# Layer 3's label masks made transposed, counted on TensorE, and scaled after the product on VectorE

## The chip, the cores and the metric

One Trainium2 chip, one core. The metric is the device time of one execution in microseconds (us). The kernel before took 1689.04 us, the median of three runs (1688.54 to 1689.13).

## The reference

A graph network of four layers runs on 64 graphs. Each graph has 128 nodes with 256 features, and an integer adjacency matrix of 128x128 that all layers share. Layers 0 and 2 are attention with eight heads, layer 1 is attention with one head, and each layer ends in a layer norm. The change is in layer 3, which sums neighbours by label, projects the sums and runs a gated unit:

```python
labels = jnp.arange(1, D + 1, dtype=adj.dtype)                  # D = 4 labels
mask = (adj[None] == labels[:, None, None, None]).astype(dt)
weight = mask / (jnp.sum(mask, axis=-1, keepdims=True) + EPS)
agg = jnp.einsum('dbmn,bnh->bmdh', weight, hid).reshape(hid.shape[0], hid.shape[1], D * H)
out = jax.nn.relu(_linear(agg, Wd, bd))
r = jax.nn.sigmoid(_linear(out, Wri, bri) + _linear(hid, Wrh, brh))
z = jax.nn.sigmoid(_linear(out, Wzi, bzi) + _linear(hid, Wzh, bzh))
n = jnp.tanh(_linear(out, Wni, bni) + r * _linear(hid, Wnh, bnh))
out = (1.0 - z) * n + z * hid                                   # then a layer norm
```

Row m of a label's mask is divided by its own sum, and this factor depends only on m. So it can be applied to the mask before the product, or to row m of the product.

## The kernel before, in words

**Rounds.** Two graphs (G = 2) are one pair, and 32 pairs run as 32 rounds of a software pipeline. Every engine has an order written out by hand (`ORDER`, with the function `periods`). An entry `lab.2@4` is part 2 of the step `lab`, run in a period for the pair that is four behind. Each engine runs its list once per period in that order, and semaphores alone tie the engines to one another. The lists of two engines may begin at different points of the round. An engine that waits holds back all that stands behind it in its list; SP's list holds the DMAs.

**Number forms.** Most products are made in fp32r, from a high and a low part of each operand, which takes three products (hi by hi, hi by lo, lo by hi). Products in plain fp32 stand in the trace as two TensorE instructions each. Transposes are products with an identity.

**Layer 3 before.** `mask` (VectorE, L990) makes the four 0/1 masks of both graphs in E3 with nodes m on partitions. `cnt` (VectorE, L995) sums rows, `guard` adds the epsilon, `rcnt` takes the reciprocal, and `wm` (GpSimd, L827) multiplies the masks by it. `wt.0` and `wt.1` transpose the weighted masks on TensorE (L577), ScalarE copies them out to wT (L740). `lab.0` to `lab.3` (TensorE, L590) multiply the node features by the label's part of Wd, for one graph and two labels each, into the banks B3 and A3 in turn; ScalarE copies each to xw (L747). `out` (TensorE, L599) multiplies xw by wT in plain fp32 and sums the four labels in bank A3; ScalarE adds the bias and applies relu (L752), and VectorE splits the result into high and low parts (L1005, L1008). `nh`, `rh`, `ri`, `ni`, `z` are the projections of the gates, and `mixt` transposes the mixed result.

**What stands around it.** `s02.0` and `s02.1` are the scores of layers 0 and 2 together (L403): four heads' worth of banks A0, B0, A2, B2 are filled at each. `s02.1` waits until ScalarE has read the four banks of `s02.0` (`exp0.1`, `exp2.1`); before that VectorE masks each bank (`fill`, L889), takes row maxima (`max`, L892, L968), and ScalarE exponentiates in four pieces (`exp`, L666, L727). `v0` projects layer 0's values, ScalarE adds their bias (L651), and `vb0` (L452) transposes them. `p0`, `p2`, `p1` transpose attention weights; `hop0`, `hop2` (L417) apply them; `back0` (L491) and `n1`, `n2`, `n3` (L391) are transposes; `vo1` and `v2` are at L385.

## Time and profile before

| | |
|---|---|
| median of 3 runs | 1689.04 us |
| the profiled execution | 1689.4 us, its span 1687.6 us |
| TensorE (PE) busy | 1619.2 us, 96% of the span |
| ScalarE (ACT) busy | 1205.6 us, 71% |
| VectorE (DVE) busy | 1130.4 us, 67% |
| GpSimd (POOL) busy | 782.0 us, 46% |
| mean granted TensorE clock | 0.985 of full speed |

The span is the time from the first to the last instruction, and the execution's time is 1.8 us longer. Busy shares are means over filling, steady rounds and draining. "PEld" is TensorE's weight load, which overlaps its products. Durations of neighbouring instructions on one engine overlap a little, so what an instruction costs in a stream is the distance from its start to the next one's start; the chain of waits gives such distances.

### The profile page before, as it was taken

Reading aid. Unit: us, or ns where it says so; the run is one execution under the profiler, and the core shown is the slowest. Engines: PE = TensorE matmul, PEld = TensorE weight load, DVE = VectorE, ACT = ScalarE, POOL = GpSimd, SP = SyncE. Lnnn points to the kernel's source line nnn. Section 1 sums busy time; section 2 is a strip of 40 time slices with the busy share of each in tenths; the row PEclk is TensorE's granted clock in tenths of the full one; section 3 lists DMA queues with packets and bytes.
Section 4 is the critical chain, followed back from the end, with each engine's and each line's share of the span. In section 5 each row is a group of like instructions: output and inputs, shape, how many; then the busy total and the mean of one; then the engine's idle time right before and its main releaser. Section 6 shows DMA issues by size and latency. Waiting matters only on the chain.

```text
span 1687.6 us, 44431 instructions
## 1 busy us (share of the span) xinstructions
PE 1619.2 (96%) x17552; PEld 1488.0 (88%) x17552; DVE 1130.4 (67%) x2875; ACT 1205.6 (71%) x4008; POOL 782.0 (46%) x774
## 2 busy tenths in 40 slices
PE   4788999999999999999999999999999999999985
PEld 3677999999999999999999999999999999999885
DVE  3566666677766676766667676666767666677642
ACT  4477777777777777777777777877778777777542
POOL 1345454534554454455544455454445554544521
PEclk8899999999999999999999999999999999999997
DMA  5000000110011111001101101111110111100000
GB/s 191 17 23 27 26 27 30 33 33 23 15 32 33 30 33 33 17 21 33 33 30 32 33 6 32 33 30 33 33 33 5 33 33 30 33 27 17 20 7 13
DMA packets 71135, 51.51 MB, mean 31 GB/s; under 512 B 4368, under 2 KB 69904, under 8 KB 70288
## 3 DMA queue, kind: packets, MB, share of 16 engines
q1 hardware_dynamic: 70928, 48.66, 9.5%
q8 instruction: 140, 2.29, 0.6%
q14 instruction: 67, 0.55, 0.1%
HBM read 40.26 MB, written 8.39 MB: 29 GB/s over the span
## 4 chain that ended last, share of the span: by engine, by line
PE 91%; issue 3%; DVE 3%; ACT 2%; POOL 1%; DMA 1%; SPq 0%; POOLq 0%; DVEq 0%; ACTq 0%
PE bank_A L373 15%; PE bank_B L373 10%; PE bank_A L599 7%; PE bank_B L590 5%; PE bank_A L590 5%; PE bank_A L417 5%; PE bank_B L417 4%; PE bank_A L403 4%; PE bank_C L411 3%; PE bank_C L373 3%; PE bank_X L373 3%; PE bank_B L385 3%; PE bank_X L385 3%; PE bank_X L525 2%; PE bank_A L391 2%
## 5 line engine op out<-in xcount | busy, mean ns | idle before, releaser
L795 POOL TENSOR_TENSOR E<-E,rsum 128x512 f32<-128x512 f32 x256 | 276.5, 1085 | 302.7 <-DVE rsum L896 181.8
L803 POOL TENSOR_TENSOR rstd<-var,minus_half 128x2 f32<-128x2 f32 x128 | 90.6, 708 | 219.4 <-DVE var L931 219.4
L373 PE MATMUL bank_A<-xT_hi,w_hi 128*128 128x256 f32 x512 | 139.4, 294 | 13.7 <-DVE xT_lo L866 11.5
L818 POOL TENSOR_TENSOR xn<-y,row 128x512 f32<-128x512 f32 x64 | 82.8, 1294 | 124.1 <-DVE y L983 122.5
L373 PE MATMUL bank_A<-xT_hi,w_lo 128*128 128x256 f32 x512 | 134.0, 283 | 0.0
L783 POOL TENSOR_SCALAR absent<-absent 128x256 int32<-128x256 int32 x64 | 57.3, 895 | 162.0 <-DMA absent<-in_adj 154.3
L889 DVE COPY_PREDICATED_SCALAR bank_A<-absent,fill 128x512 f32 x128 | 92.4, 743 | 44.7 <-PE bank_B L403 43.8
L599 PE MATMUL bank_A<-wT,xw 128*128 128x128 f32 x1024 | 119.6, 275 | 0.0
L599 PEld LDWEIGHTS bank_A<-wT,xw 128*128 128x128 f32 x1024 | 116.9, 192 | 0.0
L690 ACT ACTIVATE xT_hi<-bank_A,col 128x256 fp32r<-128x256 f32 x128 | 65.2, 561 | 71.0 <-PE bank_A L391 71.0
L964 DVE TENSOR_TENSOR vnat<-bank_B,row 128x512 f32<-128x512 f32 x32 | 22.1, 691 | 132.9 <-PE bank_B L385 132.9
L373 PEld LDWEIGHTS bank_A<-xT_hi,w_hi 128*128 128x128 f32 x512 | 97.1, 190 | 15.9 <-issue 12.0
L1005 DVE CAST oT_hi<-oT 128x512 fp32r<-128x512 f32 x32 | 14.4, 451 | 136.4 <-ACT oT L752 136.4
L373 PE MATMUL bank_A<-xT_lo,w_hi 128*128 128x256 f32 x512 | 102.9, 283 | 0.0
L417 PE MATMUL bank_A<-PT,vnat 128*32 128x128 f32 x2560 | 97.6, 279 | 4.2 <-ACT PT L672 2.7
L373 PE MATMUL bank_B<-xT_hi,w_hi 128*128 128x256 f32 x384 | 100.5, 284 | 0.0
L373 PE MATMUL bank_B<-xT_hi,w_lo 128*128 128x256 f32 x384 | 100.3, 283 | 0.0
L666 ACT ACTIVATE E<-bank_A,nmax 128x128 f32<-128x128 f32 x256 | 91.0, 380 | 13.0 <-DVE nmax L892 13.0
L373 PEld LDWEIGHTS bank_A<-xT_hi,w_lo 128*128 128x128 f32 x512 | 97.5, 190 | 1.2
L889 DVE COPY_PREDICATED_SCALAR bank_B<-absent,fill 128x512 f32 x128 | 94.9, 742 | 0.0
L417 PE MATMUL bank_B<-PT,vnat 128*32 128x128 f32 x2560 | 94.2, 274 | 0.0
L411 PE MATMUL bank_C<-ident,E 128*128 128x128 f32 x512 | 81.2, 282 | 12.5 <-POOL E L795 7.4
(197 smaller groups left out, 6018.7 us busy)
## 6 DMA issues: line engine op xcount, KB each, us to landing
...
```

The lines of the kernel that those rows point to most:

```text
L373: mm = nc.tensor.matmul(bank[:, oc * GN:(oc + 1) * GN], a, b, start=first and i == 0 and (last or oc == 0), stop=last and i == len(terms) ...
L385: mm = nc.tensor.matmul(bank[:, g * D:(g + 1) * D], a, b, start=i == 0, stop=i == len(terms) - 1)
L403: mm = nc.tensor.matmul(b[:, at:at + P], qT[hs, c, ns], kT[hs, c, ns], start=True, stop=True)
L411: mm = nc.tensor.transpose(bank[:, at:at + P], E[:, h, g, c], ident[:])
L417: mm = nc.tensor.matmul(bank[hh * HD:(hh + 1) * HD, c * P:(c + 1) * P], vnat[:, g, h * HD:(h + 1) * HD], PT[:, order.index(hh), g, c], sta ...
L590: mm = nc.tensor.matmul(BA3[part % 2][:, :], a[3][:, kc, g * P:(g + 1) * P], w[:, n:n + 2, kc, :], start=kc == 0 and j == 0, stop=kc == NC ...
L599: mm = nc.tensor.matmul(A3[:, c * GN + g * P:c * GN + (g + 1) * P], xw[:, g, d, c * P:(c + 1) * P], wT[:, g, d], start=d == 0, stop=d == L ...
L666: e = nc.scalar.activation(E0[:, part].rearrange("p g c n -> p (g c) n")[:, a], AB0[part % 2][:, a * P:(a + 1) * P], ACT.Exp, bias=nmax0[: ...
L795: nc.gpsimd.tensor_tensor(e, e, rs[:, part].unsqueeze(2).to_broadcast([P, SB, P]), ALU.mult).then_inc(e_sig.sem, 1)
L803: nc.gpsimd.tensor_tensor(rstd[part][:], var[part][:], minus_half[:], ALU.pow)\
L818: nc.gpsimd.tensor_tensor(to[:], y[part][:], rowc(f"gamma{part}"), ALU.mult)\
L889: nc.vector.copy_predicated(s, m, f).then_inc((filled0 if L == 0 else filled2).sem, 1)
```

## The change

The host also hands in a transposed copy of the adjacency, `adjt`, and layer 3's DMA reads that one. `mask` writes the masks straight into wT (nodes n on partitions) as 0/1 in fp32r, into two tiles in turn. `cnt` moves to TensorE: eight products of a mask with a tile of ones of 128x2, into B3. `guard` reads them from there. `wm`, both `wt` on TensorE and both on ScalarE go. After each `lab`, ScalarE writes the high part of xw and a new VectorE step `xlo` the low part. A new step `agg` on TensorE multiplies the mask by high and low part, for one graph and two labels, in fp32r, into the half pair of banks that `lab` has just left. A new VectorE step `acc` (eight of them) scales each label's product by its reciprocal count and sums into agg. `out` becomes four transposes of agg. All five orders are rewritten; that of the DMAs as well. `lab.2` and `lab.3` wait for the `acc` steps before them.

```diff
 ORDER = {
     "tensor": [
-        "hop0.7@1 hop2.1@3 n3@4 back0.6@1 wo2.0@3 wo2.1@3 n2@2 wt.1@4 back0.7@1 lab.0@4 lab.1@4 k0 q0 k2@2 q2@2 v2@2",
-        "n1@1 lab.2@4 s02.0 v0 lab.3@4 nh@4 vb0 l1w out@4 g1@1 s02.1 p0.0 rh@4 ri@4 p0.1 vo1@1 p0.2 ni@4 s1@1 p0.3",
-        "z@4 hop0.0 hop0.1 p2.0@2 back0.0 back0.1 p1@1 p2.1@2 hop0.2 hop0.3 o1@1 back0.2 mixt@4 back0.3 p2.2@2 hop0.4",
-        "hop0.5 p2.3@2 wt.0@3 back0.4 back0.5 hop2.0@2 hop0.6",
+        "back0.1@1 cnt@4 hop0.2@1 hop0.3@1 p2.2@3 mixt@5 back0.2@1 back0.3@1 p2.3@3 hop0.4@1 hop0.5@1 hop2.0@3",
+        "back0.4@1 back0.5@1 hop2.1@3 hop0.6@1 hop0.7@1 n3@4 wo2.0@3 wo2.1@3 back0.6@1 n2@2 back0.7@1 k0 q0 lab.0@4",
+        "lab.1@4 k2@2 q2@2 v2@2 n1@1 agg.0@4 s02.0 l1w agg.1@4 lab.2@4 v0 g1@1 lab.3@4 vo1@1 agg.2@4 s02.1 vb0",
+        "agg.3@4 s1@1 p0.0 out@4 nh@4 rh@4 ri@4 p0.1 p1@1 ni@4 p0.2 z@4 p0.3 o1@1 hop0.0 hop0.1 p2.0@2 back0.0 p2.1@2",
     ],
     "scalar": [
...
+        "t2@3 k0@1 lab.0@5 q0@1 lab.1@5 k2@3 q2@3 hi1@2 t1@2 exp0.0@1 lab.2@5 exp2.0@3 g1@2 exp2.1@3 exp0.1@1 lab.3@5",
+        "v0@1 vo1@2 vb0@1 l1w@1 split.1@1 out@5 exp0.2@1 p0.0@1 exp1@2 nh@5 exp0.3@1 p0.1@1 r@5 p1@2 x0 p0.2@1",
+        "exp2.2@3 n@5 p0.3@1 split.2@1 exp2.3@3 z@5 p2.0@3 back0.0@1 back0.1@1 split.3@1 p2.1@3 p2.2@3 back0.2@1",
+        "back0.3@1 p2.3@3 back0.4@1 back0.5@1 split.4@1 hi3@4 t3@4 hi2@2",
     ],
     "gpsimd": [
...
+        "sh.1@4 absent.2@3 pow.0@2 ne1@2 sc.1@3 sc.0@2 sc.3@6 pow.2@4 e2.0@3 e0.0@1 e0.1@1 sh.0@2 e1@2 e0.2@1 sh.3@6",
+        "e0.3@1 e2.1@3 e2.2@3 e2.3@3 absent.0 pow.3@5 pow.1@2",
     ],
     "vector": [
-        "max0.0@1 fill0.1@1 max0.1@1 l1w@1 lo1@2 max2.1@3 rec2.0@3 rec0.0@1 o_hi@5 o_lo@5 fill0.2@1 rec0.1@1 max0.2@1",
-        "fill0.3@1 agg.2@4 max0.3@1 rows@1 split.1@1 rec0.2@1 fill2.2@3 eps.2@4 max2.2@3 rec0.3@1 fill2.3@3 max2.3@3",
-        "rec2.1@3 gate@5 sum@5 max1@2 rec2.2@3 mixa@5 nrm.2@4 rec1@2 hop0.0@1 hop0.1@1 mixb@5 mixc@5 x0 hop0.2@1",
-        "rec2.3@3 hop0.3@1 y1@2 bn.3@5 agg.3@5 eps.3@5 bn.1@2 hop0.4@1 hop0.5@1 split.2@1 agg.1@2 nrm.3@5 hop2.0@3",
-        "eps.1@2 hop0.6@1 hop2.1@3 nrm.1@2 hop0.7@1 y2.0@3 lo3@4 y0.0@1 y2.1@3 y0.1@1 split.3@1 bn.0@1 agg.0@1 lo2@2",
-        "mask@3 eps.0@1 split.4@1 nrm.0@1 bn.2@3 v2@2 cnt@3 guard@3 rcnt@3 fill2.0@2 fill0.0 max2.0@2 fill2.1@2",
+        "nrm.3@6 hop2.0@4 nrm.1@3 hop2.1@4 hop0.6@2 y2.0@4 hop0.7@2 y0.0@2 lo3@5 y0.1@2 split.3@2 y2.1@4 bn.0@2 lo2@3",
+        "mask@4 bn.2@4 agg.2@4 agg.0@2 eps.0@2 split.4@2 nrm.0@2 rcnt@5 xlo.0@5 v2@3 xlo.1@5 acc.0@5 acc.1@5",
+        "fill0.0@1 max0.0@1 fill2.0@3 lo1@2 max2.0@3 acc.2@5 fill2.1@3 acc.3@5 max2.1@3 fill0.1@1 max0.1@1 l1w@1",
+        "xlo.2@5 rec0.0@1 eps.2@4 rec2.0@3 xlo.3@5 acc.4@5 acc.5@5 rec0.1@1 acc.6@5 acc.7@5 fill0.2@1 max0.2@1",
+        "fill2.2@3 max1@2 o_hi@5 o_lo@5 fill0.3@1 max0.3@1 rows@1 split.1@1 rec1@2 rec0.2@1 max2.2@3 rec2.1@3",
+        "fill2.3@3 gate@5 rec0.3@1 sum@5 max2.3@3 mixa@5 rec2.2@3 y1@2 hop0.0@1 hop0.1@1 x0 mixb@5 mixc@5 rec2.3@3",
+        "bn.1@2 hop0.2@1 hop0.3@1 bn.3@5 agg.1@2 agg.3@5 eps.3@5 hop0.4@1 eps.1@2 hop0.5@1 split.2@1 nrm.2@4 guard@4",
     ],
     "sync": [
-        "ld_adj.1@3 ld_adj.0@2 store@8 ld_adj.2@3 ld_adj.3@3 ld_x@1 ld_xt ldw@1",
+        "ld_adj.0@1 ld_adj.3@4 store@7 ld_adj.1@2 ld_adj.2@3 ld_xt ldw@1 ld_x@2",
     ],
...
+        xw_hi = over(xw, "xw_hi", [P, 2, 2, D], F32R)
+        xw_lo = over(xw, "xw_lo", [P, 2, 2, D], F32R, 16 * D)
...
-                sp.dma_start((absent, adj1, absent2, adj3)[L][:], adj_v[r]).then_inc(adj_loaded[L].sem, 16)
+                sp.dma_start((absent, adj1, absent2, adjT3)[L][:], (adjt_v if L == 3 else adj_v)[r]).then_inc(adj_loaded[L].sem, 16)
...
-                if step == "wt":
-                    wait(pe, wm_ready, it, 1)
-                    if part == 0:
-                        wait_before(pe, summed, it, 1)
-                    else:
-                        wait(pe, xt32[3], it, 1)
-                    for d in range(LABELS):
-                        mm = nc.tensor.transpose(BA3[part][:, d * P:(d + 1) * P], E3[:, d, part, :], ident[:])
-                    mm.then_inc(w_t.sem, 1)
+                if step == "cnt":
+                    wait(pe, masked, it, 1)
+                    wait_before(pe, summed, it, 1)
+                    for g in range(G):
+                        for d in range(LABELS):
+                            mm = nc.tensor.matmul(B3[:, 2 * (g * LABELS + d):2 * (g * LABELS + d) + 2], wT[it % 2][:, g, d],
+                                                  ones[:],
+                                                  start=True, stop=True)
+                    mm.then_inc(counted.sem, 1)
                 if step == "lab":
                     g, pair = divmod(part, LABELS // 2)
                     if part == 0:
                         wait(pe, xlo_ready[3], it, 1)
-                    if part < 2:
-                        wait(pe, wt_ready, it, part + 1)
-                    else:
-                        wait(pe, xw_ready, it, part - 1)
+                        wait(pe, guarded, it, 1)
+                    if part == 1:
+                        wait(pe, xt32[3], it, 1)
+                    if part >= 2:
+                        wait(pe, summed_up, it, 2 * (part - 1))
                     n = SLOT[f"d{2 * pair}"]
                     for kc in range(NC):
                         for j, (a, w) in enumerate(((xT_hi, w_hi), (xT_lo, w_hi), (xT_hi, w_lo))):
@@ -591,17 +596,20 @@
                                                   w[:, n:n + 2, kc, :], start=kc == 0 and j == 0,
                                                   stop=kc == NC - 1 and j == 2)
                     mm.then_inc(labelled.sem, 1)
+                if step == "agg":
+                    g, pair = divmod(part, LABELS // 2)
+                    wait(pe, xw_lo_ready, it, part + 1)
+                    wait(pe, masked, it, 1)
+                    for d in range(2):
+                        for xs in (xw_hi, xw_lo):
+                            mm = nc.tensor.matmul(BA3[part % 2][:, d * D:(d + 1) * D], wT[it % 2][:, g, 2 * pair + d],
+                                                  xs[:, part % 2, d], start=xs is xw_hi, stop=xs is xw_lo)
+                    mm.then_inc(agg_t.sem, 1)
                 if step == "out":
-                    wait(pe, xw_ready, it, 4)
-                    for c in range(NC):
-                        for g in range(G):
-                            for d in range(LABELS):
-                                mm = nc.tensor.matmul(A3[:, c * GN + g * P:c * GN + (g + 1) * P],
-                                                      xw[:, g, d, c * P:(c + 1) * P], wT[:, g, d],
-                                                      start=d == 0, stop=d == LABELS - 1)
-                    mm.then_inc(out_t.sem, 1)
+                    wait(pe, summed_up, it, G * LABELS)
+                    transpose_y(A3, agg).then_inc(out_t.sem, 1)
                 if step == "nh":
-                    wait(pe, xw_ready, it, 3)
+                    wait(pe, summed_up, it, G * LABELS)
                     project(B3, [("nh", xT_hi[3], xT_lo[3])]).then_inc(nh_t.sem, 1)
...
-                if step == "wt":
-                    wait(act, w_t, it, part + 1)
-                    nc.scalar.activation(wT[:, part].rearrange("p d n -> p (d n)"), BA3[part][:, :],
-                                         ACT.Copy).then_inc(wt_ready.sem, 1)
                 if step == "lab":
                     if starts(it):
                         act.wait_ge(w_split, SPLIT["5"])
-                    g, pair = divmod(part, LABELS // 2)
                     wait(act, labelled, it, part + 1)
-                    nc.scalar.activation(xw[:, g, 2 * pair:2 * pair + 2].rearrange("p d f -> p (d f)"),
-                                         BA3[part % 2][:, :], ACT.Copy).then_inc(xw_ready.sem, 1)
+                    if part >= 2:
+                        wait(act, agg_t, it, part - 1)
+                    nc.scalar.activation(xw_hi[:, part % 2].rearrange("p d f -> p (d f)"), BA3[part % 2][:, :],
+                                         ACT.Copy).then_inc(xw_hi_ready.sem, 1)
...
-                if step == "wm":
-                    wait(pool, rcnt_ready, it, 1)
-                    for g in range(G):
-                        w = E3[:, :, g, :]
-                        a = nc.gpsimd.tensor_tensor(w, w, rcnt[:, g].unsqueeze(2).to_broadcast([P, LABELS, P]),
-                                                    ALU.mult)
-                    a.then_inc(wm_ready.sem, 1)
...
                 if step == "mask":
                     wait(dve, adj_loaded[3], it, 16)
-                    wait_before(dve, w_t, it, 2)
+                    if it >= 2:
+                        wait(dve, agg_t, it - 2, SB)
                     for d in range(LABELS):
-                        a = nc.vector.tensor_scalar(E3[:, d], adj3[:], float(d + 1), None, ALU.is_equal)
+                        a = nc.vector.tensor_scalar(wT[it % 2][:, :, d, :], adjT3[:], float(d + 1), None, ALU.is_equal)
                     a.then_inc(masked.sem, 1)
-                if step == "cnt":
-                    wait(dve, masked, it, 1)
-                    for g in range(G):
-                        a = nc.vector.tensor_reduce(cnt[:, g, :, 0], E3[:, :, g, :], AX_X, ALU.add)
-                    a.then_inc(counted.sem, 1)
                 if step == "guard":
                     wait(dve, counted, it, 1)
-                    nc.vector.tensor_reduce(degree[:], cnt[:], AX_X, ALU.add).then_inc(guarded.sem, 1)
+                    count = B3[:, 0:2 * G * LABELS].rearrange("p (g d two) -> p g d two", g=G, d=LABELS)
+                    nc.vector.tensor_scalar(degree[:], count[:, :, :, 0], DEG_EPS, None, ALU.add)\
+                        .then_inc(guarded.sem, 1)
                 if step == "rcnt":
                     wait(dve, guarded, it, 1)
                     nc.vector.reciprocal(rcnt[:], degree[:]).then_inc(rcnt_ready.sem, 1)
+                if step == "xlo":
+                    wait(dve, xw_hi_ready, it, part + 1)
+                    nc.vector.tensor_tensor(xw_lo[:, part % 2].rearrange("p d f -> p (d f)"), BA3[part % 2][:, :],
+                                            xw_hi[:, part % 2].bitcast(F32).rearrange("p d f -> p (d f)"),
+                                            ALU.subtract).then_inc(xw_lo_ready.sem, 1)
+                if step == "acc":
+                    i, d = divmod(part, 2)
+                    g, pair = divmod(i, LABELS // 2)
+                    n = 2 * pair + d
+                    if part == 0:
+                        wait(dve, rcnt_ready, it, 1)
+                    if d == 0:
+                        wait(dve, agg_t, it, i + 1)
+                    if n > 0:
+                        wait(dve, summed_up, it, part)
+                    o = BA3[i % 2][:, d * D:(d + 1) * D]
+                    if n == 0:
+                        a = nc.vector.tensor_scalar(agg[:, g], o, rcnt[:, g, 0:1], None, ALU.mult)
+                    else:
+                        a = nc.vector.scalar_tensor_tensor(agg[:, g], o, rcnt[:, g, n:n + 1], agg[:, g], ALU.mult, ALU.add)
+                    a.then_inc(summed_up.sem, 1)
...
+        "adjt": v["adj"].transpose(0, 2, 1),
```

## Rows read from the trace of the kernel before

**Rows 1.** The page: busy time of engines, and the chain that ended last, by engine.
```profile
PE 1619.2 (96%) x17552; PEld 1488.0 (88%) x17552; DVE 1130.4 (67%) x2875; ACT 1205.6 (71%) x4008; POOL 782.0 (46%) x774
...
PE 91%; issue 3%; DVE 3%; ACT 2%; POOL 1%; DMA 1%; SPq 0%; POOLq 0%; DVEq 0%; ACTq 0%
```
**Rows 2.** Busy by stretch: stretch, length, then PE, PEld, DVE, ACT, POOL; PE clock.
```profile
800.00:850.00 50.00, 50.00 (x553) 46.31 (x552) 34.84 (x90) 37.26 (x125) 24.80 (x25) 1.00 0.10 28
...
1500.00:1550.00 50.00, 50.00 (x553) 46.34 (x552) 34.65 (x90) 37.35 (x127) 24.27 (x24) 1.00 0.08 23
...
1600.00:1650.00 50.00, 42.24 (x346) 38.01 (x342) 26.03 (x67) 22.69 (x69) 15.90 (x16) 0.99 0.03 11
```
**Rows 3.** Chain of waits from 800 to 855 us: start us, length us, what.
```profile
800.74 0.44 PE bank_A L623 x4
...
803.43 0.44 PE bank_B L577 x4
...
809.81 1.39 PE bank_B L590 x6
...
812.60 1.44 PE bank_A L373 x12
...
822.73 1.63 PE bank_C L373 x12
...
827.62 3.57 PE bank_A L599 x32
...
832.62 0.30 PE bank_A L403
...
841.33 0.06 PE bank_X L515
...
850.21 0.44 PE bank_A L623 x4
```
**Rows 4.** The line of `out`: ns min/median/max, first and last start in us.
```profile
L599 PE MATMUL bank_A<-wT,xw x1024: 272/275/276, 184.4 to 1667.6; 128*128 128x128 f32 x171
```
**Rows 5.** TensorE's weight loads by form: shapes, count, busy us, mean ns.
```profile
L373 PEld LDWEIGHTS bank_A<-xT_hi,w_lo 128*128 128x128 f32 x512 | 97.5, 190 | 1.2
...
L417 PEld LDWEIGHTS bank_B<-PT,vnat 128*32 128x32 f32 x2560 | 72.7, 110 | 0.2
```
**Rows 6.** VectorE's groups by form: count, busy us, mean ns, idle before.
```profile
L901 DVE SCALAR_TENSOR_TENSOR kT<-vT,bank_A 128x256 f32<-128x256 f32 x128 | 53.1, 415 | 25.6 <-PE bank_A L417 25.6
...
L995 DVE TENSOR_REDUCE cnt<-E 128x4 f32<-128x512 f32 x64 | 40.6, 675 | 0.0
...
L959 DVE TENSOR_TENSOR y<-bank_X,xn 128x512 f32<-128x512 f32 x32 | 22.1, 691 | 12.6 <-PE bank_X L525 12.6
```
**Rows 7.** VectorE in order of time behind `s02.0` and `s02.1`: start us, length us, what.
```profile
822.87 1.41 DVE L889 COPY_PREDICATED_SCALAR bank_A<-absent,fill 128x512 f32 x2 [0.73 <-PE bank_B L403]
...
834.27 0.75 DVE L889 COPY_PREDICATED_SCALAR bank_A<-absent,fill 128x512 f32 x1
834.93 0.17 DVE L896 RECIPROCAL rsum<-esum 128x4 f32<-128x4 f32 x1
835.05 0.69 DVE L892 TENSOR_REDUCE nmax<-bank_A 128x4 f32<-128x512 f32 x1
835.66 0.74 DVE L889 COPY_PREDICATED_SCALAR bank_B<-absent,fill 128x512 f32 x1
```
**Rows 8.** ScalarE in order of time: `v0`, `lab.3`, first pieces of `exp`, a last one.
```profile
824.40 0.84 ACT L651 ACTIVATE vT<-bank_C,col 128x256 f32<-128x256 f32 x2 [1.72 <-PE bank_C L373]
825.78 0.60 ACT L747 ACTIVATE xw<-bank_A 128x512 f32<-128x512 f32 x1 [0.54 <-PE bank_A L590]
826.27 0.36 ACT L727 ACTIVATE E<-bank_A,nmax 128x128 f32<-128x128 f32 x1
...
827.64 0.39 ACT L666 ACTIVATE E<-bank_A,nmax 128x128 f32<-128x128 f32 x1
...
830.28 0.28 ACT L666 ACTIVATION_READ_ACCUMULATOR E<-bank_B,nmax 128x1 f32 x1
```

26 lines of the change are left out of this document (13 added, 13 removed), and 4 rows, old and new, of the table ORDER.

## The prediction

> **What bounds the kernel now.** Read the page first: TensorE is busy 96% of the span, and the chain that ended last runs through it for 91%, while VectorE has 67% and ScalarE 71% [rows 1]. Then the stretches. From about 200 to 1550 us TensorE has no idle time at all at the full clock (1.00, the 2.4 GHz level), and in the same 50 us VectorE works 34.8 and ScalarE 37.3 us; only while the pipeline fills and drains is TensorE idle [rows 2]. So in the steady rounds time is the sum of TensorE's work and nothing else, and I take that sum from the chain of waits, where consecutive starts are what each step really costs. A round is the distance between two `mixt`: 850.21 - 800.74 = 49.47 us [rows 3]. `out` runs from 184 to 1668 us [rows 4], so 27.6 rounds, say 28, hold layer 3 while TensorE is saturated (184 to 1550 us); the other four lie in the drain.
>
> **TensorE, what goes.** Both `wt`: 2 x 0.44 us. `out`: 3.57 us for 32 instructions. Together 4.45 us per round [rows 3].
>
> **TensorE, what comes.** `agg` is 4 steps x 2 labels x 2 parts = 16 fp32r products with a 128x128 load and 256 columns. That is the form of the projections, 1.44 us for 12, so 0.12 each and 1.92 in all. The new `out` is four transposes, 0.44 us as `mixt` [rows 3]. `cnt` is eight products of two columns, each behind a load of 128 columns in fp32r; no row shows it. The nearest is a transpose, which also loads 128 columns for a short product, at 0.11 us each [rows 3]; and loads of 128 columns take 80 ns more than those of 32, 0.83 ns a column, 107 ns for 128 [rows 5]. So 8 x 0.109 = 0.87 us. From below: L515, bf16, loads 128 columns and costs 0.06 us, 0.45 in all. From above: load and product one behind the other with nothing overlapped, 190 + 275 ns [rows 4, 5], 3.72 in all. I take 0.87, the transposes' row being nearest in shape. The switches between forms cost the same as before: the step behind `s02.0` costs 0.19 extra (1.63 against 1.44 us [rows 3]), whether it is `v0` or now `agg.1`, and there are four groups of `hop` in both orders. Net: 4.45 - (1.92 + 0.44 + 0.87) = 1.22 us less in a round.
>
> **ScalarE and GpSimd.** ScalarE loses two copies of 0.5 us and keeps four for `lab`; GpSimd loses `wm` (two instructions of about 1 us). Neither is on the path, so this is worth nothing by itself. That holds for the DMAs too: `adjt` has the size of what it replaces, and in SP's new list its load waits for the `mask` of the pair before, made half a round before. It is queued behind `ld_adj.0`, which waits for `fill0.3`, and has most of a round (48 us) until the next `mask`. `store`, `ld_adj.1`, `ld_adj.2`, `ld_xt`, `ld_x` wait for steps at rising places of the same round, and what each feeds is due some 10 to 40 us behind its wait. If that cover were gone a landing, about 3 us, would show in each round.
>
> **VectorE.** It loses `cnt` (2 x 0.68 us) and gains four `xlo` (the form of L959, 0.69 us long) and eight `acc` (the form of L901, 0.42 us) [rows 6]. A VectorE instruction overlaps the next by 0.08 to 0.09 us, and one that waits for its predecessor starts 0.03 behind its end (834.27 + 0.75 = 835.02, then 835.05) [rows 7]. So an `xlo` costs 0.60 and an `acc` 0.33, or 0.45 where it waits for the one before, and a `cnt` 0.60: 4 x 0.60 + 8 x 0.39 - 2 x 0.60 = 4.3 us more, 39 of 48 us. It is no bound on the average. It is one in one stretch, and that is the term that I add.
>
> **The stretch from `s02.0` to `s02.1`.** `s02.1` refills banks that `exp0.1` and `exp2.1` must have read. Put zero at the end of `s02.0`. Before, TensorE had v0, lab.3, nh, vb0, out and g1 in between, 9.9 us (822.73 to 832.62 in rows 3), and the exps were through 7.8 us behind (830.28 + 0.28 = 830.56 [rows 8]): 2 us of slack. Now it has agg.1 0.67, lab.2 1.40, v0 1.44, g1 1.43, lab.3 1.40, vo1 1.41, agg.2 0.48: 8.23 us. VectorE goes, in its new order and at the distances of rows 7 (0.14 from the end of `s02.0` to the first fill, a fill 0.66 to the next start, a max 0.61 or a hundredth less, a max 0.03 behind the end of its own fill): fill0.0 starts at 0.14, max0.0 0.91, fill2.0 1.51, lo1 2.17, max2.0 2.78, acc.2 3.38, fill2.1 3.71, acc.3 4.37, max2.1 4.70, fill0.1 5.30, max0.1 6.07, ending at 6.76. An exp takes 1.37 us to the next one's start (826.27 to 827.64) and 1.55 to its end (two from 827.64 to 830.56 are 2.92) [rows 8]. exp2.1 (5.4 to 6.8) is just out of the way, exp0.1 ends at 8.35, and `s02.1` starts some 0.2 late. Right behind, ScalarE does `lab.3` from 8.17, `v0` from 8.66 (0.49 per copy, 825.78 to 826.27), ending at 9.50 (0.84 long [rows 8]); `vb0` waits for that and would have started at 9.33 - 0.15. So together 0.4 us per round. `lab.3` waits for `acc.3`, which ends at 4.79 when TensorE wants to start at 4.78; a loss there would lie within the same 0.4, since s02.1 waits anyway.
>
> A rule that speaks against the change bears on this stretch. The rows show that VectorE's next instruction starts before the one in front has ended: 835.05 + 0.69 = 835.74, and the next starts at 835.66 [rows 7]. The Trainium skill (VectorE: DVE Perf Modes, section "The DRAIN you can't avoid") says that the next one doesn't start until the pipe is empty. By the rows the stretch costs 0.4 us; by the rule it is longer, and rival C gives that time. The trace of before doesn't bear the rule out.
>
> Further on, with the same distances, I find these the next to be late: `p1` behind rec1 and e1 (0.1 us of slack), `z` behind ScalarE's `r` (0.1), `hop0.0` behind `p0.3` (0.1), `agg.2` behind `xlo.2` (0.2), `out` behind `acc.7` (0.4). I cost them at nothing, and each that fails costs tenths of a us per round. The new dependence of `lab.0` on `guard`, and `cnt` on `mask`, has 4 us and more.
>
> **Filling and draining.** From `k0` of a pair to its `mixt` is 235 us in both orders (four lags and 36 us; five lags of 48.6 less 8), so the pipeline is as deep. In the drain TensorE works 42 of 50 us [rows 2]; there the removed work counts in part, and the chain lab, xlo, agg, acc, out replaces lab, out at about equal length. I take 2.5 us gained for the four pairs, between -3 (lost) and 5 us.
>
> **Sum.** -1.22 x 28 = -34.2; +0.4 x 28 = +11.2; -2.5. Together -25.5 from the profiled execution's 1689.4 us: 1663.9. That execution lies 0.4 above the median of the runs (1689.04), so 1663.5, rounded to 1664 us.
>
> **The rivals.**
> A. The forecast: TensorE sheds 1.22 and gives 0.4 back at `s02.1` and `vb0`. 1664 us.
> B. No stall: the distances on VectorE and ScalarE are a few hundredths shorter than I put them, and TensorE stays saturated. For it: not one wait in the steady rounds before. Against: 8.35 + latency is over 8.23 by the best rows. 1664 - 11 = 1653 us; with counts at the lower end (0.42 less per round) 1641.
> C. VectorE sets the pace of the stretch. If nothing overlaps, eight of its starts move by 0.08 to 0.09 us each, 0.7 in all; with the 0.4, 1.1 us stall in 1.22 saved. 1664 + 0.7 x 28 = 1684 us. The same time follows if the places with 0.1 to 0.2 of slack all fail. For it: 39 of 48 us busy, and waits in order. Against: the overlap in rows 7.
> D. The counts. If load and product of a two-column matmul don't overlap and nothing else does, `cnt` costs 3.72 instead of 0.87: 1664 + 2.85 x 28 = 1744 us, slower than before. It turns the sign when one count costs over 0.22 us ((0.87 + 0.82)/8 = 0.21, the drain's gain included). For it: no row has a product that short. Against: every load in the trace overlaps the product in front.
> E. The change doesn't bring its saving because fp32r products with the mask as the loaded side run as two instructions. The twelve instructions of a projection and the six of a `lab` [rows 3] are its products one for one, so fp32r takes one each; so I give it almost nothing (it would add 1.9 us a round, 1718 us).
>
> **How the numbers follow.** A 0.52, B 0.20, C 0.20, D and E 0.08. What can't be told from no change is within 0.2%, 3.4 us. A and B are faster; of C, most is faster (1684 is 5 us below), a part is the same, and a little slower, where more than one place fails. Faster 0.84, same 0.06, slower 0.10. The range runs from 1649 (B with a little of the cheap counts) to 1684 (C), and leaves out the ends of B and C, and D: about 2 in 10. The spread inside A, 0.2 to 0.7 of stall and 0.6 to 1.3 for the counts, is 1656 to 1676.
>
> **What would show it.** Right: line groups of `agg` at a step of 0.12 per product and 16 per round, `out` as four transposes of 0.11, `cnt` at 0.11 each, a round of 48.6 to 48.7 us between two `mixt`, and TensorE waits in steady rounds for `exp0.1` (L666) and for `v0`'s bias (L651), 0.2 each, where there were none. Wrong: `cnt` at over 0.15 each; a round at 48.3 without waits (B); or TensorE waiting for `summed_up`, `xw_lo` or softmax steps over 0.6 us in a round (C).

## The result: 0.25% slower, and the profile after

The kernel after takes 1693.75 us (median of eight runs, 1693.39 to 1694.62), beside 1689.12 us (eight runs, 1687.52 to 1692.0) for the kernel before on the same chip: a ratio of 1.0025, with 1.0015 to 1.0035 as its 95% interval. 1664 us were forecast, with a range up to 1684. The profiled execution took 1693.96 us, its span is 1692.2.

The page of the kernel after, busy time by engine and the chain that ended last by engine, against [rows 1]:

```profile
PE 1610.3 (95%) x17168; PEld 1456.4 (86%) x17168; DVE 1261.9 (75%) x3195; ACT 1172.9 (69%) x3944; POOL 706.5 (42%) x710
...
PE 83%; ACT 6%; DVE 5%; issue 4%; POOL 1%; DMA 0%; POOLq 0%; SPq 0%; DVEq 0%; ACTq 0%
```

TensorE's share of the chain falls from 91 to 83%; ScalarE's rises from 2 to 6% and VectorE's from 3 to 5%. The chain now leaves TensorE. In the busy times by stretch (columns as in [rows 2]) the steady rounds hardly show it, because a product is recorded as longer (0.28 us) than the distance to the next one (0.12), and so covers a short wait:

```profile
800.00:850.00 50.00, 49.93 (x558) 45.53 (x547) 39.64 (x102) 36.24 (x123) 22.91 (x24) 1.00 0.11 31
```

VectorE has gone from 34.8 to 39.6 us of 50, where 39 of 48 were forecast. The chain of waits of one round (start us, length us, what), against [rows 3]:

```profile
800.96 0.44 PE bank_A L631 x4
...
808.94 1.62 PE bank_A L377 x12
...
817.66 1.43 PE bank_B L389 x12
...
819.11 0.69 DVE vnat L962
819.80 0.24 DVE xw_lo L1001
...
820.32 0.49 DVE agg L1016
...
820.83 0.38 DVE agg L1018
...
821.25 0.77 DVE bank_A L887
...
822.04 0.70 DVE nmax L890
...
823.03 1.24 ACT E L674 x7
824.27 0.49 ACT xw_hi L752
824.76 1.40 ACT E L735 x8
826.16 0.53 ACT qT L704
826.69 1.40 ACT E L735 x8
...
828.32 1.25 ACT E L674 x7
829.57 0.49 ACT xw_hi L752
830.05 0.74 ACT vT L659 x2
...
830.84 0.66 PE bank_C L456 x4
...
838.66 0.43 PE bank_X L524 x2
...
840.96 2.92 PE bank_A L377 x24
...
847.66 0.79 PE bank_B L579 x8
...
850.05 0.44 PE bank_A L631 x4
```

Before, this stretch was TensorE alone, and every row of the chain was a PE row. Now the chain leaves it when `v2` is through (819.09), goes over VectorE (`v2`, `xlo.1`, `acc.0`, `acc.1`, `fill0.0`, `max0.0`), then over ScalarE (four banks of exps with the copies of `lab.2` and g1 between them, `lab.3`, `v0`), and comes back at `vb0` (830.84). A round is 850.05 - 800.96 = 49.09 us, where 48.65 was forecast.

**Where the 4.6 us of span are.** I take the starts of `mixt` for all 32 pairs. "Steady" are the 27 distances between the first 28 of them (24 of them 49.47 before, 25 of them 49.09 to 49.11 after).

| | before | after | difference |
|---|---|---|---|
| fill: start to the first `mixt` | 206.98 | 211.51 | +4.53 |
| steady: 27 rounds | 1335.86 | 1325.69 | -10.17 |
| drain: the last four distances | 40.66, 34.80, 28.80, 31.52 | 40.43, 38.31, 32.80, 34.45 | +10.21 |
| end: last `mixt` to the end | 8.98 | 9.01 | +0.03 |

So the change does make a round 0.38 us shorter. It pays that back, and more, at the two ends.

**The clock at the two ends.** In the steady rounds both kernels have the full clock (1.00, the 2.4 GHz level). At the ends they don't, and not in the same measure. First two stretches of the fill, of the kernel after and of the one that copies 2 columns of g1 (below); then the stretch from `out` to `mixt` of the last pair but one, in the kernel after and in the one without the low part; then the same of the last pair in both (the granted share stands third from the end of a row):

```profile
90.00:170.00 80.00, 64.38 (x788) 55.12 (x788) 49.62 (x122) 55.65 (x207) 35.94 (x36) 0.94 0.09 26
...
90.00:170.00 80.00, 64.94 (x803) 55.94 (x802) 51.97 (x128) 56.61 (x211) 34.37 (x35) 0.96 0.09 26
...
1635.59:1648.74 13.15, 11.56 (x84) 11.47 (x84) 4.58 (x7) 4.26 (x10) 0.00 (x0) 0.87 0.01 2
...
1625.67:1637.33 11.66, 10.06 (x84) 9.98 (x84) 4.58 (x7) 4.28 (x10) 0.00 (x0) 1.00 0.01 1
...
1670.02:1683.19 13.17, 10.78 (x76) 10.58 (x77) 4.58 (x7) 4.26 (x10) 0.00 (x0) 0.87 0.00 1
...
1656.91:1668.56 11.65, 9.27 (x77) 9.07 (x77) 4.58 (x7) 4.28 (x10) 0.00 (x0) 1.00 0.01 1
```

These two kernels do the same work from `out` to `mixt`, and it takes 11.65 or 11.66 us at the full clock and 13.15 or 13.17 where the granted share is 0.87. In the kernels that bear on it ("at 1.2 GHz" is the granted share of the fill from 17 us on, turned into us at that level):

| | first `mixt` | at 1.2 GHz before it | third distance of the drain, of it `out` to `mixt` | last distance, of it `out` to `mixt` |
|---|---|---|---|---|
| before | 206.98 | 34.1 | 28.80, 14.43 | 31.52, 14.43 |
| after | 211.51 | 37.6 | 32.80, 13.15 | 34.45, 13.17 |
| `nh` ahead of `out` | 211.22 | 37.5 | 31.06, 11.36 | 34.34, 11.35 |
| without the counts | 208.46 | 30.7 | 30.92, 11.65 | 34.32, 13.19 |
| `acc` small | 209.00 | 30.8 | 29.77, 11.66 | 33.10, 11.65 |
| both small | 209.16 | 34.2 | 29.77, 11.65 | 31.62, 11.65 |
| without the low part | 210.75 | 37.5 | 29.02, 11.66 | 31.23, 11.65 |

So 3.0 us of the drain's 10.2 are TensorE at its lower level in the third and the last distance. Of the fill's 4.5 us some 1.8 at most are (3.5 us more at half speed); that is an estimate from this table. Each kernel has one trace, so how far these stretches scatter from run to run isn't known. The runs on record allow a rough check by the mean granted share: at 0.982 or 0.983 seven runs of the kernel before (beside the experiments) took 1689.48 to 1692.3 us and seven of the kernel after 1693.39 to 1694.62. So the clock is a part of the 4.6 us and not the whole. What brings the clock down at `out` stays open: TensorE waits 1.65 us for `acc` in front of it in the kernel after (1635.59) and 1.29 without the counts (1621.55), where it doesn't fall.

### The profile page after: what moved, and what is told of

It is laid out like the page before. It is cut to its first block, busy times and chain, and to the rows that moved or that the text cites. A ratio compares the mean times of both kernels' runs of the same rounds, so it can differ in the third digit from the quotient of the medians.

```text
span 1692.2 us, 44108 instructions
## 1 busy us (share of the span) xinstructions
PE 1610.3 (95%) x17168; PEld 1456.4 (86%) x17168; DVE 1261.9 (75%) x3195; ACT 1172.9 (69%) x3944; POOL 706.5 (42%) x710
## 4 chain that ended last, share of the span: by engine, by line
PE 83%; ACT 6%; DVE 5%; issue 4%; POOL 1%; DMA 0%; POOLq 0%; SPq 0%; DVEq 0%; ACTq 0%
PE bank_A L377 16%; PE bank_B L377 10%; PE bank_A L421 5%; PE bank_A L595 5%; PE bank_B L595 4%; PE bank_B L421 4%; PE bank_C L415 3%; PE bank_A L407 3%; PE bank_B L389 3%; PE bank_A L395 3%; PE bank_A L415 2%; PE bank_A L495 2%; ACT E L735 2%; PE bank_C L377 2%; PE bank_X L389 2%
## 5 line engine op out<-in xcount | busy, mean ns | idle before, releaser
L800 POOL TENSOR_TENSOR E<-E,rsum 128x512 f32<-128x512 f32 x256 | 263.5, 1040 | 208.1 <-DVE rsum L970 149.3
L674 ACT ACTIVATE E<-bank_A,nmax 128x128 f32<-128x128 f32 x256 | 90.5, 371 | 44.8 <-DVE nmax L890 44.8
L421 PE MATMUL bank_A<-PT,vnat 128*32 128x128 f32 x2560 | 103.4, 280 | 2.7 <-ACT PT L743 1.4
L377 PE MATMUL bank_B<-xT_hi,w_hi 128*128 128x256 f32 x384 | 104.4, 293 | 0.5 <-issue 0.5
L421 PE MATMUL bank_B<-PT,vnat 128*32 128x128 f32 x2560 | 101.0, 276 | 0.0
L936 DVE TENSOR_SCALAR y<-y,mv,rstd 128x256 f32<-128x256 f32 x192 | 79.7, 455 | 27.0 <-POOL rstd L808 27.0
L962 DVE TENSOR_TENSOR vnat<-bank_B,row 128x512 f32<-128x512 f32 x32 | 22.1, 692 | 100.1 <-PE bank_B L389 100.1
L735 ACT ACTIVATE E<-bank_A,nmax 128x128 f32<-128x128 f32 x256 | 94.8, 442 | 0.8 <-DVE nmax L966 0.8
L674 ACT ACTIVATE E<-bank_B,nmax 128x128 f32<-128x128 f32 x256 | 92.9, 409 | 0.0
L680 ACT ACTIVATE PT<-bank_C 128x512 f32<-128x512 f32 x128 | 83.8, 654 | 11.4 <-PE bank_C L415 11.2
L752 ACT ACTIVATE xw_hi<-bank_B 128x512 fp32r<-128x512 f32 x64 | 38.6, 604 | 75.7 <-PE bank_B L595 75.7
```

The lines of the kernel that those rows point to most:

```text
L377: mm = nc.tensor.matmul(bank[:, oc * GN:(oc + 1) * GN], a, b, start=first and i == 0 and (last or oc == 0), stop=last and i == len(terms) ...
L421: mm = nc.tensor.matmul(bank[hh * HD:(hh + 1) * HD, c * P:(c + 1) * P], vnat[:, g, h * HD:(h + 1) * HD], PT[:, order.index(hh), g, c], sta ...
L674: e = nc.scalar.activation(E0[:, part].rearrange("p g c n -> p (g c) n")[:, a], AB0[part % 2][:, a * P:(a + 1) * P], ACT.Exp, bias=nmax0[: ...
L680: nc.scalar.activation(PT0[:, part].rearrange("p g c n -> p (g c n)"), C0[:, :], ACT.Copy, scale=1.0 - ALPHA).then_inc(pt0_ready.sem, 1)
L735: e = nc.scalar.activation(E2[:, part].rearrange("p g c n -> p (g c) n")[:, a], AB2[part % 2][:, a * P:(a + 1) * P], ACT.Exp, bias=nmax2[: ...
L800: nc.gpsimd.tensor_tensor(e, e, rs[:, part].unsqueeze(2).to_broadcast([P, SB, P]), ALU.mult).then_inc(e_sig.sem, 1)
```

## Experiments

Ratios are to the kernel before on the same chip, with 95% intervals. "Round" is the steady distance between two `mixt`. The kernels start from the kernel after, which has a round of 49.09, a first `mixt` at 211.51 and a drain (the last four distances together) of 145.99 us; one, named below, starts from the kernel before. Those with 2 columns, without counts or without the low part leave work out, and their times are for measuring alone.

### Which engine holds the stretch: `acc` alone

```diff
-                    o = BA3[i % 2][:, d * D:(d + 1) * D]
+                    o = BA3[i % 2][:, d * D:d * D + 2]
...
-   a = nc.vector.tensor_scalar(agg[:, g], o, rcnt[:, g, 0:1], None, ALU.mult)
+   a = nc.vector.tensor_scalar(agg[:, g, 0:2], o, rcnt[:, g, 0:1], None, ALU.mult)
...
```

> Each acc works on 2 of its 256 columns, so layer 3's sum is left out but for those; TensorE's work is the same, VectorE does some 2 us less in a round. Theory A (VectorE's longer list makes s02.1, vb0, k0 and p1 late, some 0.8 us per round over TensorE's own sum of 48.3): the steady round between two mixt falls from 49.09 to 48.5 or 48.6, the time from 1693.8 to some 1676. Theory B (TensorE's own work was sized too low, waits are small): the round stays at 49.0 to 49.1 and the time within 4 us of 1693.

1684.5 us, 0.9968 [0.9955, 0.9981]; round 49.03, first `mixt` 209.00, drain 140.35. VectorE lost some 1.9 us of work in a round (38.74 to 36.87 us of 49.1), and the round shortened by 0.06. The expected 48.5 to 48.6 is refuted: `acc` alone doesn't hold the round. Its chain goes over ScalarE (start us, length us, what):

```profile
819.31 0.04 ACT E L674
...
820.81 0.49 ACT xw_hi L752
...
824.63 1.40 ACT E L674 x8
```

From 819.31 ScalarE works in one row to 826.03 (the exps of four banks and, between them, the copies of `lab.2` and g1), and TensorE waits for it at `s02.1`. Most of the 9 us of time came from the ends: 2.5 from the fill and 5.6 from the drain. Not all of that is `acc`: this kernel also had 6.8 us less at the lower clock in its fill and none of it between `out` and `mixt` (table above).

### ScalarE alone

```diff
-  nc.scalar.activation(flat(qT1), X1[:, :], ACT.Copy).then_inc(q1_ready.sem, 1)
+  nc.scalar.activation(flat(qT1)[:, 0:2], X1[:, 0:2], ACT.Copy).then_inc(q1_ready.sem, 1)
```

> ScalarE copies 2 of 512 columns of g1's result (layer 1's queries are left out but for those): 0.4 us less on ScalarE between s02.0 and s02.1, VectorE and TensorE unchanged. Theory S (in that stretch the pace is ScalarE's: one fill and one max, then four exps of 1.39 and the copies of lab.2 and g1, 8.3 us): s02.1 comes 0.2 to 0.4 earlier behind s02.0, and the round falls from 49.09 to 48.7 or 48.8. Theory V (the pace is VectorE's, max0.1 releases exp0.1): s02.1 and the round stay within 0.1. With acc_small VectorE was relieved of 2.4 us and the round fell by 0.06.

1691.6 us, 1.0010 [0.9999, 1.0020]; round 49.13, first `mixt` 208.20, drain 145.44. The copy is some 0.4 us shorter and nothing is gained: now VectorE holds the same stretch. The chain of this kernel:

```profile
818.36 0.77 DVE bank_A L888
...
821.70 0.39 DVE agg L1019
...
822.75 0.38 DVE agg L1019
...
827.95 0.66 PE bank_C L456 x4
```

From `fill0.0` to `vb0` it is 9.59 us both here (818.36 to 827.95) and in the kernel after (821.25 to 830.84). There `acc.2` and `acc.3` lie beside ScalarE's chain; here they are in it.

### Both at once

> `acc` works on 2 of its 256 columns and ScalarE copies 2 of 512 columns of g1; the columns left out are zero. Theory S (between s02.0 and vb0 VectorE's chain and ScalarE's chain are about equally long, so that relieving one gains nothing and relieving both gains): the round falls from 49.09 by 0.3 to 0.5 us, to 48.6 to 48.8, time about 1677 us. Rival F (the stretch isn't what holds the round; what is gained there comes back at k0, p1, z whatever engine is relieved): 49.0 as in the two single runs, about 1687 us.

1673.0 us, 0.9903 [0.9888, 0.9917]; round 48.65, as expected of two engines that are jointly tight. Two edits worth 0.06 and -0.04 alone are worth 0.44 together. The chain of waits stays on TensorE through the whole stretch:

```profile
809.90 1.42 PE bank_B L389 x12
...
822.70 0.58 PE bank_C L456 x4
...
830.45 0.22 PE bank_X L524 x2
...
832.56 3.13 PE bank_A L377 x24
...
849.83 1.62 PE bank_A L377 x12
```

From the end of `v2` (811.32) to `vb0` it is 11.38 us, against 11.75 in the kernel after (819.09 to 830.84), and `vb0` itself is 0.58 instead of 0.66. That is the 0.44. `p1` (L524) no longer waits, 0.22 instead of 0.43, but `z` (the 24 products) takes 3.13 instead of 2.92: the 0.21 moved. `k0` keeps its 1.62. It waits for `y0.0`, with which VectorE reads the bank of `back0.6`, and that step ended only 0.66 us earlier.

### The other waits, by order alone

```diff
-  n3@4 wo2.0@3 wo2.1@3 back0.6@1 n2@2 back0.7@1 k0 ... ri@4 p0.1 p1@1 ni@4 p0.2
+  n3@4 wo2.0@3 back0.6@1 wo2.1@3 back0.7@1 n2@2 k0 ... ri@4 p0.1 ni@4 p1@1 p0.2
```

> TensorE's order alone: back0.6 ahead of wo2.1 and back0.7 ahead of n2, so that y0.0 and y0.1 are done when k0 and q0 come, and p1 behind ni. Nothing is left out. Theory A': k0's 0.18 us and p1's 0.21 us per round go, the round falls from 49.09 to 48.7, the time to some 1683. Rival (these waits only take up slack that would come back at s02.1 or z): the round stays over 49.0.

1696.33 us, 1.0038 [1.0023, 1.0053]; round 49.20. `k0` falls to 1.43 and `p1` to 0.22 as meant, and the waits return at `back0.6` and at `z` (3.13). The expected 48.7 is refuted and the rival was right.

The same together with both reliefs and with `nh` ahead of `out` (below):

> As the kernel before this one (acc on 2 of 256, g1's copy on 2 of 512 columns), and TensorE's order has back0.6 ahead of wo2.1, back0.7 ahead of n2, p1 behind ni, nh ahead of out. Theory S: with the stretch relieved, the waits at k0 (0.18) and p1 (0.21) are the ones left, and giving them cover now keeps: 0.3 less than both_small, 48.3 to 48.5 a round, about 1668 us. Rival F: again no less than both_small, the waits show at z, back0.6 and hop0.0.

1674.71 us, 0.9914 [0.9899, 0.9929]; round 48.67, not the 48.3 to 48.5 of theory S. `k0` is 1.44, `p1` 0.22, but `z` is 3.11 and `back0.6` 0.44 instead of 0.22. So the stretch was held by the two engines together, but what is left beyond it wasn't moved away by these order edits.

### Less work for TensorE: without the counts

```diff
-        "back0.1@1 cnt@4 hop0.2@1 ...
+        "back0.1@1 hop0.2@1 ...
```

> The eight count products and guard and rcnt are left out; a constant stands in for the reciprocals. They lie between back0.1 and hop0.2, where TensorE waits for nothing. Theory A' (TensorE's own work plus waits of fixed size at s02.1, vb0, k0 and p1): the round falls by all of cnt, 49.09 to 48.3, the time to some 1671. Rival (the round is held by a loop over other engines that runs all round it, so TensorE's work can be cut without gain): the round falls by less than 0.3.

1680.41 us, 0.9941 [0.9926, 0.9956]; round 48.71, first `mixt` 208.46, drain 144.00. `guard` and `rcnt` go with them, a constant stands in. The counts are 0.79 us in the chain, and leaving them out gives 0.38, which lies between the two expectations. In the chain of this kernel `hop0.2`, which lost its cover, waits for ScalarE's copy (L685):

```profile
839.83 0.28 ACT vnat L685
```

It starts at 840.16 and takes 0.65 us instead of 0.57.

### Without the low part of xw

```diff
-                        for xs in (xw_hi, xw_lo):
+                        for xs in (xw_hi,):
```

> The low part of xw is left out: no xlo on VectorE, agg has 8 products instead of 16. TensorE's own work falls by 0.96 us per round, VectorE's by 2.4. Theory A': the round falls by 0.5 to 0.9 (the two agg steps in front of s02.0 and behind s02.1 count in full, those in the stretch, where ScalarE's four exps and two copies take 8.3 us, not). Theory D1 on the drain (the last pairs are paced by layer 3's latency from n3 to the next n3, in which each xlo stands with 0.6 to 0.7): the last two distances fall from 32.8 and 34.5 by 1.5 to 3 us each. Theory D2 (only the order counts): they stay within 0.5.

1678.71 us, 0.9932 [0.9918, 0.9947]; round 48.90, last four distances 39.94, 37.59, 29.02, 31.23. TensorE has 0.96 us less in a round, VectorE four `xlo` of 0.60, and the round gives 0.19, where 0.5 to 0.9 were expected. The drain gives 8.2 us: its last two distances are back near those of before (28.80 and 31.52). 3.0 us of this are the clock, which stays full from `out` to `mixt` here, as before.

With both reliefs as well:

> No xlo, agg with the high part alone (8 products: TensorE 0.96 us less in a round), acc on 2 of 256 columns, g1's copy on 2 of 512. Alone, leaving out the low part gave 48.90 a round. Theory S: with both engines relieved the round falls well under that, to 48.0 to 48.4 us, time about 1655 us. Rival F: 48.8 to 48.9, the waits move behind s02.1 instead, about 1677 us.

1662.05 us, 0.9833 [0.9817, 0.9850]; round 48.37. This is between the theories: 0.28 below the kernel with both reliefs and the low part, of 0.96 taken from TensorE. The chain is back on ScalarE, from 811.98 to 819.48, with exps and the copies of `lab.2` and `lab.3` in one row. By the chain the next bound is ScalarE; that wasn't tried.

### Before's arithmetic in the new orders

The cut below is against the kernel after; the arithmetic is that of the kernel before.

```diff
-  "... cnt@4 ... agg.0@4 s02.0 l1w agg.1@4 ... agg.2@4 s02.1 vb0 agg.3@4 ..."
+  "... wt.0@4 ... wt.1@4 ... s02.0 l1w ... s02.1 vb0 ..."
```

> The arithmetic of the kernel before (masks with nodes m on partitions, cnt on VectorE, wm on GpSimd, wt, fp32 out) in the changed kernel's orders, with wt.0 at cnt's place, wt.1 before back0.7 and the agg, xlo and acc steps taken out. Theory D1 (the new arithmetic lengthens layer 3's chain): fill and drain are nearly those of before (first mixt at 207 us, last four distances 136 us), steady round 49.4 to 49.8, time 1685 to 1700. Theory D2 (the new orders cost it): first mixt near 211 us and the last four distances near 143 us or more, time 1700 to 1710.

1763.89 us, 1.0440 [1.0423, 1.0458]; round 51.56, first `mixt` 214.93, last four distances 45.38, 39.84, 28.67, 31.15. Both expectations missed the time: with the old arithmetic put in this way, the new orders are far slower. What it tells: with the old arithmetic the last two distances are close to those of before (28.80, 31.52). So the 6.9 us that these two have lost come in with the new arithmetic, 3.0 of them by way of the lower clock. The second distance and the fill are as long or longer with the old arithmetic: they don't come from the new one alone. This kernel's rounds are 2.5 us longer, though, so its fill and its first two distances are a weak comparison.

### `nh` ahead of `out`

```diff
-  agg.3@4 s1@1 p0.0 out@4 nh@4 rh@4 ri@4
+  agg.3@4 nh@4 out@4 s1@1 p0.0 rh@4 ri@4
...
-                    wait(pe, summed_up, it, G * LABELS)
+                    wait(pe, summed_up, it, 6)
```

> nh waits for acc.5 instead of acc.7 and stands before out, both before s1 and p0.0. Nothing is left out. Theory D1 (the last pairs run one behind the other through layer 3, and the time from n3 to mixt of one pair is what grew in the drain, 1.5 us of it because nh now stands between out and rh): the last four distances between mixt shrink from 146.0 by 1.2 to 1.5 us for each of the last three, 4 in all; the steady round may grow by 0.2 to 0.5 as s1 and p1 come later. Theory D2 (the drain's 10 us come from the rotated order as a whole, not from layer 3's chain): the last four distances stay within 1 us of 146.0.

1690.64 us, 1.0003 [0.9994, 1.0012]; round 49.06, drain 144.43. Its drain is 1.6 us shorter, where 4 were expected, and even that can't be put down to `nh`: the third distance gives 1.74 (31.06), but without the counts it is as short (30.92) with `nh` in its old place; both have the full clock there. The kernel is the best one that leaves nothing out: as fast as the kernel before, not faster. Together with the order edit for `k0` and `p1` it is 1694.37 us, 1.0026 [1.0016, 1.0036], round 49.18, so that expectation failed too:

> k0_p1 and nh_first together: nh waits for acc.5 and stands before out, both before s1 and p0.0. Nothing is left out. Round as in k0_p1, 48.7 (the later p1 no longer waits), the last four distances between mixt 144 instead of 146, the time to some 1680: below both kernels.

### Moving `agg` and `acc`

Earlier (`agg.0`, `agg.1` and four `acc` ahead of `v2`):

```diff
-  k2@2 q2@2 v2@2 n1@1 agg.0@4 s02.0 l1w agg.1@4 lab.2@4
+  k2@2 q2@2 agg.0@4 agg.1@4 v2@2 n1@1 s02.0 l1w lab.2@4
```

> agg.0 and agg.1 move ahead of v2, and acc.0 to acc.3 into VectorE's idle time before v2, out of the stretch from s02.0 to s02.1. Nothing is left out. Theory A: 1.1 us less on VectorE behind s02.0, so lab.3's wait and most of the waits at s02.1 and vb0 go: the round falls from 49.09 to 48.6 to 48.75, the time to 1680 to 1684. Theory B: the round stays at 49.1.

1724.43 us, 1.0205 [1.0190, 1.0220]; round 50.13. VectorE in order of time: `v2` (L962) stands behind four `acc`, 0.52 from start to start.

```profile
829.35 0.48 DVE L1016 TENSOR_SCALAR agg<-bank_B,rcnt 128x256 f32<-128x256 f32 x1 [1.84 <-PE bank_B L605]
...
831.39 0.68 DVE L962 TENSOR_TENSOR vnat<-bank_B,row 128x512 f32<-128x512 f32 x1
```

Later, `agg.2` behind `s02.1` with the copy of `lab.2` behind `exp0.1` (and `xlo.2` behind `rec2.0`):

```diff
-  vo1@1 agg.2@4 s02.1 vb0 ... exp0.0@1 lab.2@5 exp2.0@3 g1@2 exp2.1@3 exp0.1@1 lab.3@5
+  vo1@1 s02.1 agg.2@4 vb0 ... exp0.0@1 exp2.0@3 g1@2 exp2.1@3 exp0.1@1 lab.2@5 lab.3@5
```

> agg.2 moves behind s02.1, and with it ScalarE's copy of lab.2 behind exp0.1 and xlo.2 behind rec2.0. Nothing is left out. Theory S: the stretch loses 0.48 on TensorE and 0.49 on ScalarE, s02.1 starts 0.45 earlier, and TensorE's wait before vb0 is filled with agg.2; the round falls to 48.7 to 48.9, the time to some 1685. Theory V: VectorE's list in the stretch is as long as before, so no gain, 49.0 to 49.2.

1710.86 us, 1.0126 [1.0108, 1.0144]; round 49.75. With `nh` ahead of `out`:

> agg2_late and nh_first together. Round 0.2 to 0.4 below 49.09, the last four distances 144, the time 1680 to 1685, below both kernels. If xlo.2, acc.4 and fill0.2 get into each other's way on VectorE behind s02.1, the round stays at 49.1 and the time at 1690.

1718.06 us, 1.0167 [1.0152, 1.0183]; round 49.97. And `agg.0` behind `s02.0` with `acc.0`, `acc.1` between the fills:

```diff
-  n1@1 agg.0@4 s02.0 l1w agg.1@4
+  n1@1 s02.0 agg.0@4 l1w agg.1@4
```

> agg.0 moves behind s02.0, acc.0 and acc.1 between the first fills and maxima. Nothing is left out. TensorE gets 0.48 us more work in the stretch in which it waits for ScalarE (Theory S), and VectorE starts fill0.0 at once behind s02.0 instead of 0.25 later. Theory S: the wait at s02.1 goes and s02.0 waits 0.2 for v2; the round falls to 48.8 to 49.0. Theory V: acc.0 and acc.1 lengthen VectorE's list in the stretch by 1 us: the round grows by 0.3 to 0.8.

1813.5 us, 1.0733 [1.0710, 1.0755]; rounds of 52.34 and 53.85 in turn. `lab.2` waits for `acc`, by the groups of TensorE (busy, mean ns | idle before, and its releasers):

```profile
L595 PE MATMUL bank_B<-w_hi,xT_hi 128*128 128x512 f32 x128 | 56.4, 440 | 78.6 <-DVE agg L1018 74.2 <-DVE xT_lo L942 4.4
```

All three places that were tried for `agg` and `acc` made the round longer.

## Why the prediction was wrong, by its own steps

**TensorE's sum was right.** 1.22 us less in a round was predicted. `agg` is 0.48 per step and `out` 0.44, as worked out; the counts are 0.79 for eight instead of 0.87. Taking the measured waits (below) out of 49.09 leaves 48.19, so TensorE shed 1.28. Rivals D and E fall with it: no count costs over 0.10 us, and `agg` has the projections' step.

**The steps that failed.** Two steps of the sum failed: "I cost them at nothing" in the steady rounds, and in filling and draining "at about equal length". The first cost 12.8 us of the error, the second 17.3; the next paragraphs take them in turn.

**The stall in the stretch was right in size, wrong in how it comes about.** 0.4 us were predicted at `s02.1` and `vb0`; lifting it experimentally gave 0.44. The prediction put 2 us of slack into the kernel before; that was a misreading. The row at 830.28 in [rows 8] is the end of `exp0.1`, but `exp2.1` came behind it. ScalarE in order of time in the kernel before:

```profile
830.38 0.44 ACT L727 ACTIVATE E<-bank_B,nmax 128x128 f32<-128x128 f32 x1
...
831.65 0.30 ACT L727 ACTIVATION_READ_ACCUMULATOR E<-bank_B,nmax 128x1 f32 x1
```

So it had 0.67 us (831.95 to `s02.1` at 832.62 [rows 3]), in a stretch from which the change takes the 3.57 us of `out`. And the prediction named `acc` in VectorE's list as the cause; in the kernel after the last wait is ScalarE's, and VectorE's is as long. An `acc` is 0.48 us long (0.415 was taken from L901 in [rows 6]) and 0.51 from start to start in a chain, where 0.45 was put. Independent neighbours still overlap in the kernel after (a max from 822.04 to 822.73, the next fill from 822.65), so these records show no wait of an independent instruction for the one in front. The rule of the Trainium skill (VectorE: DVE Perf Modes, section "The DRAIN you can't avoid"), by which the next instruction doesn't start before the pipe is empty, isn't borne out by them; the same section says that one that is not held starts earlier, and these records agree with that.

**"I cost them at nothing" failed.** Of the places with little slack, `p1` and `z` did fail, each a little; `hop0.0`, `agg.2` and `out` didn't in the steady rounds. In one round of the kernel after: `k0` 1.62 instead of 1.44, `p1` 0.43 instead of 0.22, `z` 2.92 instead of the 2.85 before. With the stretch that is 0.44 + 0.18 + 0.21 + 0.07 = 0.90 us of waits, not 0.4. `k0` wasn't on the prediction's list at all: in the new order it stands 0.66 us behind the end of `back0.6`, whose bank VectorE must read first. Rival C named this, but for `k0` ("if the places with 0.1 to 0.2 of slack all fail"). The 0.90 are over the 0.6 us of waits that the prediction named as the sign of C. By span, 28 rounds of -0.82 were predicted, -22.96 us, and 27 rounds of -0.38 measured, -10.17: 12.8 us of the error.

**Filling and draining failed worst.** -2.5 us were predicted with 3 us lost as the worst; +14.8 us were measured, 17.3 us of the error and enough to change the sign. The step that failed is "the chain lab, xlo, agg, acc, out replaces lab, out at about equal length". In the drain pairs hardly overlap: `n3` of the last pair starts 4.0 us behind the `mixt` of the one before (1652.73 behind 1648.74), so a step of one pair's layer 3 is hidden by little else. TensorE in order of time, the last pair, first the kernel before:

```profile
1664.18 3.73 PE L599 MATMUL bank_A<-wT,xw 128*128 128x128 f32 x32
...
1678.62 0.66 PE L623 MATMUL bank_A<-ident,oT 128*128 128x128 f32 x4 [2.38 <-DVE oT L1029]
```

and the kernel after:

```profile
1656.57 0.79 PE L595 MATMUL bank_B<-w_hi,xT_hi 128*128 128x512 f32 x1 [2.75 <-DVE xT_lo L942]
...
1662.60 0.39 PE L605 MATMUL bank_A<-xw_hi,wT 128*128 128x256 f32 x1 [0.95 <-DVE xw_lo L1001]
...
1668.00 0.39 PE L605 MATMUL bank_A<-xw_hi,wT 128*128 128x256 f32 x1 [0.67 <-DVE xw_lo L1001]
1670.02 0.95 PE L395 MATMUL bank_A<-ident,agg 128*128 128x128 f32 x4 [1.28 <-DVE agg L1018]
...
1683.19 0.66 PE L631 MATMUL bank_A<-ident,oT 128*128 128x128 f32 x4 [2.38 <-DVE oT L1046]
```

From `lab.0` to `out` it is 13.45 us, where it was 9.27 (1654.91 to 1664.18): TensorE waits for `xlo` at `agg.1` and `agg.3` (0.95 and 0.67), for `acc` at `lab.2` and at `out` (0.17 and 1.28). `out` itself gives 2.8 us back (0.99 us to the relu instead of 3.78). From the relu to `mixt` it is 12.18 instead of 10.66. Of these 1.5 us `nh`, which now lies between, costs 0.30: with the same order the kernels without the low part and with both reliefs take 10.96 there, and 0.69 instead of 0.99 from `out` to the relu. The rest is the clock. Pairs of fp32r products take 0.63 us in the kernel after behind `out` and 0.40 a little later:

```profile
1671.62 0.63 PE L377 MATMUL bank_B<-xT_lo,w_hi 128*128 128x256 f32 x2
...
1673.96 0.40 PE L377 MATMUL bank_A<-xT_lo,w_hi 128*128 128x256 f32 x2
```

So of the 6.9 us of the last two distances, 3.9 are the longer chain and 3.0 the lower clock. The chain is shown: the kernel without the low part shortens it and the one with the old arithmetic restores the old one, and both come back near before's 28.80 and 31.52, with before's clock in these stretches. Whether the chain's own waits bring the clock down isn't shown.

The other 3.5 us of the drain (its second distance, 34.80 to 38.31, at the full clock in both) stand in every kernel, at 37.6 to 41.2, with the old arithmetic at 39.84 (granted share 0.96); they go with the new orders, and which entry costs them wasn't tried. In the chain of the kernel after, ScalarE works on exps from 1597.93 to 1600.72, then copies `lab.3`, and `xlo.3` and four `acc` follow one by one before `out` starts at 1604.01; before, TensorE's own work runs on to `out` at 1603.61. The kernels with `acc`, the copy of g1 or the counts relieved have their first `mixt` 2.4 to 3.3 us earlier (208.2 to 209.2), but they also had 3.4 to 7.0 us less at the lower clock before it, at up to half a us for each; so these gains can't be put down to the relief. What lengthened the fill, beyond the 1.8 us at most that the clock gives, stays open.

Taken together, of the 14.8 us at the ends 3.9 are layer 3's longer chain, 3.0 and at most 1.8 more the clock, and the rest, over 6, is not traced to a step.

**What a saving on TensorE is worth now.** The runs give a rate: 0.79 us less on TensorE gave 0.38 (the counts), 0.96 less gave 0.19 (the low part), and 0.28 where both other engines were relieved. The prediction counted each us of TensorE as a us of time, less one stall that it could see. Its count of TensorE's work came out; what another us of it is worth did not.
